# Padding of the expert tiles: stored ahead of time and masked, or stored once the counts are known

## The reference

```python
def _L0_ffn_ref(x, up, gate, down, router, w_up_s, w_gate_s, w_down_s):
    logits = x_ @ router.T
    idx = jnp.argmax(logits, axis=-1)
    onehot = jax.nn.one_hot(idx, router.shape[0], dtype=x.dtype)
    u = jnp.einsum('bc,ehc->ebh', x_, up)
    g = jnp.einsum('bc,ehc->ebh', x_, gate)
    h = jax.nn.silu(g) * u
    ye = jnp.einsum('ebh,ech->ebc', h, down)
    y = jnp.einsum('ebc,be->bc', ye, onehot)
    ys = jax.nn.silu(x_ @ w_gate_s.T) * (x_ @ w_up_s.T) @ w_down_s.T
    return (y + ys).reshape(b, t, c)

x = x + _L0_attn_ref(_layernorm(x), ...)
x = x + _L0_xattn_ref(_layernorm(x), ctx_1024, ctx_1024, ...)
x = x + _L0_ffn_ref(_layernorm(x), ...)
```

## Time and profile before

| | |
|---|---|
| median of 3 runs | 754.22 us (752.98 to 756.46) |
| the profiled execution: time | 756.46 us |
| the profiled execution: span, first to last instruction | 754.4 us |
| mean granted clock of TensorE | 0.972 |
| busy: PE, DVE, ACT, POOL | 712.6, 540.6, 533.2, 530.1 us |
| DMA | 27.61 MB, 37 GB/s in the mean |

### The profile page before, as it was taken

One profiled execution on the slowest core, in us unless ns is written; L12 is line 12 of the kernel. 1 busy time (PEld: TensorE's weight loads), 2 busy tenths in 40 slices (PEclk: granted clock), 3 DMA queues, 4 the chain that ended last, 5 costly groups with the idle time before them and its releaser, 6 DMA issues. The chain is left out here.

```text
span 754.4 us, 31316 instructions
## 1 busy us (share of the span) xinstructions
PE 712.6 (94%) x11673; PEld 592.2 (79%) x11673; DVE 540.6 (72%) x1406; ACT 533.2 (71%) x1943; POOL 530.1 (70%) x875
## 2 busy tenths in 40 slices
PE   6889999999999999999999999999999998699990
PEld 4577788888888888888888888888888887577560
DVE  2466777777777777777787888778777776457660
ACT  2267777877777777888887877777778777555550
POOL 3266676777777877888777777777777777456554
PEclk7799999999999999999999999999999999899995
DMA  6000000211111000000000000000000000241420
GB/s 239 4 18 9 10 10 13 69 38 38 38 39 38 17 18 26 24 25 24 25 25 24 24 25 25 25 24 25 25 32 10 11 10 10 58 127 55 128 63 16
DMA packets 22802, 27.61 MB, mean 37 GB/s; under 512 B 3448, under 2 KB 18684, under 8 KB 22656
## 3 DMA queue, kind: packets, MB, share of 16 engines
q1 hardware_dynamic: 19152, 17.80, 7.8%
q0 software_dynamic: 2784, 6.56, 2.4%
q10 hardware_dynamic: 720, 1.26, 0.5%
HBM read 16.82 MB, written 9.24 MB: 35 GB/s over the span
## 5 line engine op out<-in xcount | busy, mean ns | idle before, releaser
L1123 ACT ACTIVATE PX<-P,mx 128x128 f32<-128x128 f32 x512 | 186.0, 415 | 10.1 <-DVE mx L704 10.1
L1406 POOL TENSOR_TENSOR PX<-PX,mx 128x512 f32<-128x512 f32 x128 | 130.6, 1040 | 13.5 <-DVE mx L709 13.3
L1123 ACT ACTIVATION_READ_ACCUMULATOR PX<-P,mx 128x1 f32 x512 | 130.6, 255 | 0.0
L643 DVE TENSOR_REDUCE nmf<-P 128x4 f32<-128x512 f32 x128 | 79.4, 682 | 17.5 <-PE P L226 17.5
L704 DVE TENSOR_REDUCE mx<-P 128x4 f32<-128x512 f32 x128 | 82.9, 669 | 2.6 <-PE P L326 2.6
L1132 ACT ACTIVATE PT<-P 128x512 f32<-128x512 f32 x128 | 69.7, 599 | 20.3 <-PE P L339 20.3
L1401 POOL TENSOR_TENSOR rq<-rq,tq 128x1024 f32<-128x1024 f32 x32 | 75.8, 2369 | 2.9 <-DVE tq L668 2.9
L1396 POOL TENSOR_TENSOR rk<-rk,tk 128x1024 f32<-128x1024 f32 x32 | 75.9, 2372 | 0.0
L1366 POOL CAST nm<-nmf 128x16 bf16<-128x16 f32 x32 | 6.4, 199 | 98.0 <-DVE nmf L643 98.0
L291 PE MATMUL P<-wvT,cxT 128*128 128x512 f32 x128 | 70.8, 635 | 0.4 <-ACT nmT L1080 0.4
L1087 ACT ACTIVATE PS<-P 128x512 f32<-128x512 f32 x128 | 66.5, 614 | 3.8 <-PE P L247 3.7
(11 more groups left out here) (179 smaller groups left out, 1831.4 us busy)
## 6 DMA issues: line engine op xcount, KB each, us to landing
ew<-in_ew SPq DMA_DIRECT2D x9, 384.0 KB, 3.7
xrow<-z_xs SPq DMA_DIRECT2D x24, 136.0 KB, 2.1
z_xs<-c SPq DMA_DIRECT2D x16, 136.0 KB, 3.0
x<-in_x SPq DMA_DIRECT2D x32, 64.0 KB, 2.0
cxT<-in_ctxT SPq DMA_DIRECT2D x31, 64.0 KB, 1.8
wk<-z_xs SPq DMA_DIRECT2D x6, 136.0 KB, 2.1
wvT<-z_xs SPq DMA_DIRECT2D x6, 136.0 KB, 2.1
tab<-in_tab SPq DMA_DIRECT2D x1, 512.0 KB, 7.5
```

What stands on the lines that cost most here:

```text
L643: dve.tensor_reduce(nmf[b % 2][:, 0, r, :], v3(bank(f"s{r}")), AX.X, ALU.max, negate=True).then_inc(S["v_bm"][r], 1)
L1123: t = act.activation(PX[(4 * b + r) % 6][:, c, :], p[:, c * 128:c * 128 + 128], ACT.Exp, bias=m[:, 0, r, c:c + 1], scale=1.0, accum_out=m[ ...
L1406: pool.tensor_tensor(X[:, :, :], X[:, :, :], mx[b % 3][:, 2, r, :].rearrange("p (h a) -> p h a", a=1).to_broadcast([128, 4, 128]), ALU.mul ...
```

## The change

Padding is no longer stored into each expert's region ahead of time. `nobody` keeps the eight blocks of padding. When the last batch is counted, DVE writes the end of each expert's rows to `padr` (in `f_pos`, for batch 31), and SP stores `fill` behind each of them (`pads`, offset 8, which is behind the loads of chunk 0): eight register loads and eight DMAs. `load_r(21)` now waits for these eight as well. Regions start at their first row again. `over`, `lim`, `step`, `table_limits` and the mask leave, and with them the addition and its wait in `x_send`, and the last steps of `table_rows`. `table_rows(1)` moves one round up, to `j` = 16. For chunk 0, `table_sums` now stands at the end of `f_pos` of batch 27 and `table_experts` at offset 8, both ahead of the two `d_ox` of their period; `table_rows(0)` stays behind them. `f_first` leaves: the scatter of batch 27 goes where the others go.

```diff
             def f_pos(b):
@@ vector @@
                 dve.tensor_reduce(f[:, 8:9], f[:, 0:8], AX.X, ALU.add).then_inc(S["v_pse"], 1)
+                if b == NB - 1:
+                    dve.scalar_tensor_tensor(out=padr[:, :], in0=experts, scalar=float(128 * CAP), in1=bank("pos")[:, 8:16],
+                                             op0=ALU.mult, op1=ALU.add).then_inc(S["v_pad"], 1)
                 if b + 1 in (FIRST[1], NB):
                     dve.tensor_copy(cnt[:, 0:8], bank("pos")[:, 8:16]).then_inc(S["v_cnt"], 1)
+                if b + 1 == FIRST[1]:
+                    table_sums(0)
...
-            def table_limits():
...
                 if c == 1:
-                    dve.tensor_scalar(exf[:, MOST:MOST + T], exf[:, MOST:MOST + T], cnt[:, 32:33], 128.0, ALU.add,
-                                      ALU.mult).then_inc(S["v_own"], 1)
-                    dve.wait_ge(S["v_own"], own())
-                    dve.scalar_tensor_tensor(out=exr[:, t0:t0 + T], in0=exf[:, 0:T], scalar=lim[:, 0:1],
-                                             in1=exf[:, MOST:MOST + T], op0=ALU.add, op1=ALU.min).then_inc(S["v_ex"], 1)
...
+                    dve.tensor_scalar(exr[:, t0:t0 + T], exf[:, MOST:MOST + T], cnt[:, 32:33], 128.0, ALU.add,
+                                      ALU.mult).then_inc(S["v_ex"], 1)
...
@@ pool @@
-            def f_first(b):
-                if b == FIRST[1] - 1:
-                    send(b)
-
             def f_send(b):
-                if b != FIRST[1] - 1:
-                    send(b)
-
-            def send(b):
...
             def x_send(j):
-                k, index = j - TILE0[1], xrow[j % XR][:, ID:ID + 1].bitcast(U32)
-                if k >= 0:
-                    if k == 0:
-                        pool.wait_ge(S["v_over"], 1)
-                    pool.wait_ge(S["d_xr"][j % 12], 16 * (j // 12 + 1))
-                    pool.tensor_tensor(over[:, k:k + 1], over[:, k:k + 1], index, ALU.add).then_inc(S["p_own"], 1)
-                    pool.wait_ge(S["p_own"], own())
-                    index = over[:, k:k + 1]
                 pool.wait_ge(S["v_xy"], j + 1)
...
@@ sync @@
+            def pads(b):
+                if b == NB - 1:
+                    sp.wait_ge(S["v_pad"], 1)
+                    for e in range(NE):
+                        row = sp.value_load(padr[0:1, e:e + 1], min_val=128 * CAP * e, max_val=128 * (CAP * e + CAP - 1))
+                        sp.dma_start(A["z_xs"][bass.ds(row, 128), :], fill).then_inc(S["d_pad"], 16)
...
                 e = s - 18
-                if 0 <= e < 2 * NE:
-                    k = 128 * (NE * CAP + e if e < NE else CAP * (e - NE))
+                if 0 <= e < NE:
+                    k = 128 * (NE * CAP + e)
...
+                if j == TILE0[1]:
+                    sp.wait_ge(S["d_pad"], 16 * NE)
```

More of the change, by code:

```diff
@@ L93, in build @@
         exr = sb("exr", [128, NT], U32)
-        cnt = sb("cnt", [128, 76])
-        cmpb = sb("cmpb", [128, 8 * MOST + 32])
-        over = sb("over", [128, NT], U32)
+        cnt = sb("cnt", [128, 56])
+        cmpb = sb("cmpb", [128, 8 * MOST])
+        padr = sb("padr", [128, NE], U32)
         exf = sb("exf", [128, 2 * MOST])
@@ L153, in build @@
         rtT, experts, ids = c2[:, 592:600], c2[:, 600:608], c2[:, 608:640].bitcast(U32)
-        behind, tiles = c2[:, 640:640 + MOST], c2[:, 640 + MOST:640 + 2 * MOST]
+        steps, tiles = c2[:, 640:640 + MOST], c2[:, 640 + MOST:640 + 2 * MOST]
         ewf = ew[:, 0:NE, :].rearrange("p e n -> p (e n)")
@@ L399, in f_pos @@
                 until = [(S["v_pse"], b + 1)]
+                if b == NB - 1:
+                    until.append((S["v_pad"], 1))
                 if b + 1 in (FIRST[1], NB):
@@ L799, in table_experts @@
                 t0, T = TILE0[c], TILES[c]
-                c3, cw = table(c)
+                c3 = cmpb[:, 0:8 * T].rearrange("p (j e) -> p j e", e=NE)
                 dve.wait_ge(S["v_own"], mine[0])
@@ L840, in table_rows @@
             def table_rows(c):
                 t0, T = TILE0[c], TILES[c]
-                c3, cw = table(c)
+                c3 = cmpb[:, 0:8 * T].rearrange("p (j e) -> p j e", e=NE)
                 dve.wait_ge(S["v_own"], mine[0])
-                dve.tensor_reduce(exf[:, MOST:MOST + T], cw, AX.X, ALU.add).then_inc(S["v_own"], 1)
+                dve.tensor_reduce(exf[:, MOST:MOST + T], c3, AX.X, ALU.add).then_inc(S["v_own"], 1)
                 dve.wait_ge(S["v_own"], own())
-                dve.tensor_tensor(exf[:, MOST:MOST + T], exf[:, MOST:MOST + T], behind[:, 0:T], ALU.add).then_inc(S["v_own"], 1)
+                dve.tensor_tensor(exf[:, MOST:MOST + T], exf[:, MOST:MOST + T], tiles[:, 0:T], ALU.add).then_inc(S["v_own"], 1)
@@ L1019, in _ @@
                 batch(f_pos, s - 8)
+                batch(f_experts, s - 8)
                 batch(a_v, s - 2)
@@ L1456, in x_send @@
                 pool.indirect_dma_start(
-                    out=A["out"], out_offset=bass.IndirectOffsetOnAxis(ap=index, axis=0),
+                    out=A["out"], out_offset=bass.IndirectOffsetOnAxis(ap=xrow[j % XR][:, ID:ID + 1].bitcast(U32), axis=0),
                     in_=yst[j % 8][:, :], in_offset=None, bounds_check=128 * NB - 1,
@@ L1547, in _ @@
                 batch(f_pos, s - 7)
-                batch(f_first, s - 7)
                 batch(b_rstd, s - 2)
@@ L1662, in _ @@
                 batch(first_r, s - 9)
+                batch(pads, s - 8)
             for j in range(TILE0[1], NT):
```

37 lines of the change are left out of this document (7 added, 30 removed).

## The result

| | before | with the change |
|---|---|---|
| median of 16 runs, same chip | 754.92 us (751.96 to 757.84) | 759.94 us (756.04 to 763.23) |
| ratio, with its 95% interval | | 1.0065 (1.0044 to 1.0086) |
| the profiled execution: time / span | 756.46 / 754.4 us | 759.91 / 757.8 us |
| mean granted clock of TensorE | 0.972 | 0.980 |

The change makes the kernel slower by 4.9 us (3.3 to 6.5). The forecast had it slower by 3.0, at 757.2, and called that "the same"; the measured loss lies inside its range, but just beyond the half per cent (the interval of the ratio begins at 0.44%). Parts 1 and 3 came close. In Part 2 the step that the table "costs nothing" did not, and it is the main subject here; Part 4 came out at about half.

What follows compares the result with a forecast made beforehand. The prediction took a POOL backlog to bound the kernel's end, and PE before it. Its terms, -7.7 + 4.3 + 3.4 + 3.0 = +3.0, against the median of 754.22 gave 757.2 us, range 752.5 to 760.2.

Steps and rivals of the forecast that it cites:

- Part 1, the sends: Tail on POOL: without the index addition and its wait, sends follow PE for the last 18 tiles; a gain of 7.7.
- Part 2, the scatter behind PX: POOL before tile 0: batch 27's scatter goes behind batch 31's first PX multiplication, delaying tile 0; a loss of 4.3.
- Part 2, the table: VectorE before tile 0: chunk 0's table, moved ahead of the oX additions, fits into idle time and costs nothing.
- Part 3, the late padding: SP behind the last count: eight padding stores, 1.24 apart, landing in 3.0, delay tile 21; a loss of 3.4.
- Rival (a): SP between 691 and 704: late stores slower than forecast, 0.2 more each and landing 3.8; +5.2, 759.4; chance 0.20.
- Part 4, the clock: PE behind the stall at tile 21: clock at half rate for 6.2; a loss of 3.0, ends 0 and 3.5.
- Rival (b): PE at tile 21: the clock doesn't fall; -3.0, time 754.2; chance 0.16.
- (c): POOL before tile 0: the late scatter is hidden, so 4.3 leaves the sum; 752.9; chance 0.07.
- (d): At tiles 0 and 21: Rival (b) and (c) both hold; 749.9, faster; chance 0.06.
- (e): Tail on POOL: sends held by an earlier send's landing, staying 2.0 apart, so 7.7 isn't gained; 764.9; chance 0.03.

Runs made afterwards that it cites:

- both back: The changed kernel with the chunk-0 table put back behind the oX additions and batch 27's scatter ahead of PX; 754.71 us, ratio 0.9962 to before.
- The mask addition on VectorE: The kernel before, with only the addition of the mask to a tile's indices moved from POOL to VectorE; 750.56 us, ratio 0.9909 to before.

## Why the prediction was right or wrong

**Part 1, the sends** (-7.7): right. -7.6 in the changed kernel; -7.5 of backlog and -6.9 us of time (-4.9 to -8.9) where it was done alone.

**Part 2, the scatter behind PX** (+4.3): right by itself. The forecast had 0.45 in it that the early table gives back, as VectorE's maxima no longer stand behind the table; without it, it is 4.7, to be set beside the 4.4 to 4.6 of the profile with the table back. In the changed kernel that gain came: the maxima start 0.04 behind the scores.

**Part 2, the table** (0): this is the step that failed. "The table moved ahead of that place costs nothing" took 2.37 for the table from the earlier trace rows and set it beside 2.36 of idle time. Both rows were read rightly, but a duration was carried to another place as if it belonged to the instruction alone. There POOL's rk and rq additions run, and two instructions of the table wait for them: 0.65 + 2.28 in place of 0.33, 2.6 more. The first oX addition came 2.5 late, PE's scores started 2.06 late, after a wait of 3.19 in place of 1.15, and at the lower clock they took 1.6 longer (3.70 for 2.07). Less the 0.4 of the maxima that is +3.3 at PX, and +3.4 was measured at tile 0 against the kernel with the table back. The sentence that the cover was "just wide enough" was the warning: a cover of 2.36 over 2.37 should have had an upper end to its cost, and it got 0.1. The range of Part 2 ended at 4.6, and 8.0 was measured. The experiments also show what the forecast did not see, that the two halves of Part 2 depend on each other: the early table alone costs nothing that shows (0.9998, 0.9982 to 1.0014), since it eats idle time that the scatter's chain leaves. With the scatter chained behind PX, and so behind those scores, it costs 3.4 at tile 0 and some 2.6 (0.3 to 4.9) in the ratios.

**Part 3, the late padding** (+3.4): right in sum, +3.6 from the last count to tile 21, by errors that cancel, which is luck. The issues of the eight stores start between 698.00 and 708.02, and the last takes only 0.01 (the median of the eight is 0.33), so they went 10.0/7 = 1.43 apart, not 1.24, 1.3 more in all. The last landed in 2.2, not 3.0, and the first went out 0.98 behind the start of the sum, not 1.3. The pitch wasn't even: in the chain above, two stores without disturbance are 1.13 apart (698.00 and 699.13), and twice some of SP's instructions, register moves among them, took about 0.7 each (701.72). Rival (a) had its place right and the +0.2 a store as well, though the register loads themselves took 0.28 at most; its landing of 3.8 was wrong.

**Part 4, the clock** (+3.0): the mechanism was right and the size off, by about half. The stretches of the changed kernel at the second stall:

```profile
713.00:714.00 1.00, 0.57 (x2) 0.49 (x3) 0.00 (x0) 0.23 (x1) 0.48 (x1) 0.90 0.41 115
714.00:716.00 2.00, 2.00 (x5) 0.97 (x5) 0.00 (x0) 0.39 (x2) 0.00 (x0) 0.50 0.45 128
...
717.00:718.00 1.00, 1.00 (x4) 0.51 (x4) 0.15 (x1) 0.48 (x2) 0.06 (x1) 0.89 0.49 133
```

The clock was at 0.50 from about 713.8 to 717.2, 3.4 in place of 6.2, and PE's way from tile 21 to the last tile was 1.4 longer. In "both back" the same way was 2.5 longer (37.1 against 34.6), and the clock was at 0.50 for 5.7 of it. In both, the loss is a little less than half of the time at the low clock (at half rate PE, which was busy throughout, loses half). The row of tile 0, with its 6.2, was carried over as if the low clock always lasted as long. The comparison is loose, though: four of the five other kernels without late padding, whose clock stayed at 1.00 there, took 35.7 to 35.8 for this way as well. In those four ScalarE waited 1.9 for something remote at about 708, which the profile of before doesn't have. So beside before the term is 1.4 to 2.5, inside its bounds of 0 to 3.5, and its price in the time isn't shown more closely. Rival (b), a clock that holds, did not occur.

**What no step had:** the stretch from tile 0 to the last count was 1.1 longer. PE waited 1.20 there for ACT, and ACT 1.26 for something that the trace names only as remote; the profile of before doesn't show such a wait. But that of "The mask addition on VectorE" does, where no instruction ahead of tile 21 is changed. The first line is from the changed kernel, the second from that one:

```profile
696.69 0.38 ACT L1142 ACTIVATE xhT<-P 128x256 f32<-128x256 f32 x1 [1.26 <-remote]
...
691.00 0.38 ACT L1180 ACTIVATE xhT<-P 128x256 f32<-128x256 f32 x1 [1.25 <-remote]
```

There the stretch took 40.4, against 36.95 before and 38.1 with the change. So the +1.1 lies within what this stretch differs by from profile to profile, and nothing ties it to the change. What the wait is for, no trace shows.

**Rivals (c), (d) and (e)** are out: the late scatter was not hidden, and POOL was freed.

The sum, with the terms as measured and without that +1.1: -7.6 + 8.0 + 3.6 + 1.4 = +5.4, beside +4.9 (3.3 to 6.5) in the ratio. The forecast had +3.0. That it lies as near as that is in part luck: the table's 3.4 was missing, and Part 4 had 1.6 too much.

## What to carry to other kernels

An instruction's duration belongs to its place: before moving small VectorE work with two SBUF inputs, or a `tensor_scalar` from SBUF to SBUF, look what POOL runs at the new place, and give the cost up to the end of POOL's instructions as its upper end. Where a row's cover is as wide as what it has to hide, to a hundredth, the cost is not zero but unknown. And if an engine is the backlog for 0.79 of waiting for itself, moving that one small operation to an engine with slack (0.15, and -6.9 us here) is to be tried before the data structure around it is redesigned.

## What was not expected of the hardware

- A VectorE instruction on 8 elements a partition took 2.28 to 2.34 while POOL added 1024 elements a partition, and 0.17 with one input from PSUM beside the same addition. `tensor_reduce` and a copy from PSUM at the same place were not slowed (0.16).
- After the stall at tile 21 the low clock lasted 3.4 in the changed kernel and 6.8 (705.9 to 712.7) in "both back", for stalls of 3.83 and 3.45. (In "both back" the first 1.0 of it lay in the stall itself.) Here its cost could be told to 1 or 2 us, not better.
- Some SP instructions that move a register took 0.7 in place of 0.02 to 0.15, several in a row, twice within the ten microseconds of the eight stores. What they wait for, the trace doesn't show.
- A wait of ScalarE for something "remote" of 1.2 to 1.3 stands at 690 to 697 in six of the eleven profiles, with and without the change, and in neither of two others. Such a wait in one profile should not be put down to a change before other kernels have been looked at.
- The stretch ahead of the first count took 114.0 to 117.6, with the same instructions in it but for two small memsets in two of the kernels. Two profiles must be compared from a common event on, not from the start of the span.
